# Register attention: the maxima are cut up straight behind the fourth one, and six kept products leave the similarity chain

## The chip, the cores and the metric

The kernel runs on one core of one Trainium2 chip. The metric is the device time of one execution in microseconds (us): the median of three executions of the kernel before was 1886.83 us (1886.52 to 1889.33). A core has five engines with an instruction queue each. TensorE (PE in the profile; PEld are its weight loads) multiplies matrices into PSUM banks. VectorE (DVE), ScalarE (ACT) and GpSimd (POOL) work on rows of 128 partitions. SyncE (SP) issues the large transfers. Each queue is worked off in the written order, and the queues meet only at semaphores.

## The reference, cut to what matters

The model is a four-layer decoder on 16 sequences of 128 tokens with 128 features and 16 heads of 8 features. The change lies in one of thirteen blocks, the "ffn" of layer 0, which is an attention with 5 register tokens (B is 16 and N is 128 here):

```python
qkv = (x @ W_qkv).reshape(Bx, Nx, 3, H, D)
q, k, v = (qkv[:, :, 0], qkv[:, :, 1], qkv[:, :, 2])
...
sim = (qg_n[None, None] * q_n).sum(-1).mean(-1)
sim = (sim - sim.min()) / (sim.max() - sim.min())
pos = sim > 0.9
logits = jnp.einsum('bqhd,bkhd->bhqk', q * scale, k)
...
reg_out = (x_pos[:, :REG] + x_neg[:, :REG]) * 0.5
tok_out = jnp.where(pos[:, :, None, None], x_pos[:, REG:], x_neg[:, REG:])
```

Each token is similar or not to one given query, after a minimum and a maximum over all tokens of all sequences. Each ordinary token attends to the registers and the tokens of its own side. The registers attend to both sides separately, and the two results are averaged. So no score of this block can be masked before the similarities of all 16 sequences are known.

## The kernel before, in words

All 16 sequences stay in SBUF. The blocks follow one another; each has one function per engine (`satt_pe`, `satt_act`, `satt_dve`, `satt_pool` for the five attention blocks, called with the block's name), and the order on every engine is written out by hand.

**The similarity chain** (`sim_pe`, `sim_act`, `sim_pool`, `sim_dve`) stands between the block before (cross-attention, S_X0) and the register attention (S_REG). The sequences form four groups of four. For each group TensorE turns x, multiplies it by the query weights, and ScalarE, GpSimd and VectorE make squares, products and sums of them. After the last group VectorE has the mean similarities; then a ping-pong of small operations between VectorE and TensorE follows. TensorE turns the columns (L1468), turns the extremes (L1471), spreads them to all partitions (L1474), and turns the masks (L1481). VectorE's step ahead of each adds one to `sim_mid`, TensorE's answer adds one to `sim_rows`. The masks end in `side_T` (L1623).

**Kept products.** q, k and v of all sequences are computed once by group: three products per group (`keep(g, m)`), each one PSUM bank of 128x512, which ScalarE copies to SBUF (L1503, semaphore `kept_sb`). L1451 is the form with one 512-column product (q and k, the weights standing still), L1454 the one with four 128-column products (v). Products 0 to 5 belong to groups 0 and 1 (sequences 0 to 7), 6 to 11 to groups 2 and 3. TensorE's queue mixes products 6 to 11 with the small operations of the chain, and ScalarE copies them in the same order. Two banks take turns, so product c waits for the copy of product c-2. GpSimd then spreads each group's queries of the registers into `reg_rows` (L1537).

**The attention loop** (`att_steps`, k from -2 to 17) works on several sequences at a time. In step k TensorE first multiplies the cut-up maxima of sequence k (`maxima_T`, L665, which waits for `m_cut`), computes the turned scores (L671, L675), turns the register row of k+1 (L748), subtracts the maxima (`fold_T`, L690, waits for ScalarE's copy `m_rows`, L811), computes the scores of k+1 (L644, L653), the values of k (L703), and so on down to the output projection of k-1 (L732, L358).

VectorE's step ends with the maxima of k+1 (four L873), and in this block alone with a register part: it waits for `reg_ps`, masks the register values (L912, L914), takes the register maximum (L920) and scales it (L922), for which ScalarE's exponential of the register rows (L847) waits. The next step begins with `cut_up(k)` (L879, L881): the four maxima are written as a bf16 number and its bf16 remainder, and `m_cut` is raised. ScalarE's step begins with the copy `m_rows` (L811); the register exponential stands last in its step, ahead of the next step's `m_rows` copy.

GpSimd makes the masked queries of sequence k+2 (`wides`, L537, after the values of k), a side mask (`side`, L548), and one exponent per sequence (L544).

Of the kernel before, what the change touches and what calls it, by code (L numbers as in the profile page):

```python
# [26 lines left out]
ALU = mybir.AluOpType  # L27
# [104 lines left out]
def decoder(nc, x_tok, x_T, ctx_tok, ctx_T, mask, mask_row, w_early, w_late, w_last, w_rest, bias, cols, rows,  # L132
            const, out, last=S_MOE):
    ctx = ExitStack()
    with ctx:
# [387 lines left out]
        def satt_pool(pool, sub, kind):  # L523
# [31 lines left out]
            for k in att_steps():  # L555
                if sub == S_MQA and has(k + 1):
                    wides(k + 1)
                if has(k - 2):
                    finish(k - 2)
                    if sub == S_X0 and k - 2 >= BATCH - 2:  # L560
                        sim_product(pool, k - BATCH)
                if sub != S_MQA and has(k + 2):
                    wides(k + 2)
                if sub == S_REG and has(k + 4):
                    side(k + 4)

        def satt_pe(pe, sub, kind, W, name, bias_name, mask_kind, out_w=384, out_name=None):
# [95 lines left out]
            def maxima_T(n):  # L663
                pe.wait_ge(m_cut, of_run(st, n))
                nc.tensor.matmul(ps[(n + 1) % 2][2][:, 0:128], m_cols[n % 2][:, :], ident_b[:, :], start=True,  # L665
                                 stop=True, skip_group_check=True).then_inc(mT_ps, 1)
# [70 lines left out]
            def reg_scores(n):  # L737
# [6 lines left out]
                                        skip_group_check=True)  # L744

            def reg_turn(n):
                pe.wait_ge(reg_e, n + 1)
                nc.tensor.transpose(ps[n % 2][1][:, 128:128 + REG_ROWS], reg_(n, "x")[0:REG_ROWS, :],  # L748
                                    ident[0:REG_ROWS, 0:REG_ROWS]).then_inc(reg_T, 1)
# [7 lines left out]
            for k in att_steps():  # L757
# [27 lines left out]
                if sub == S_REG and k + 1 < BATCH:  # L785
                    if has(k + 1):
                        mm = reg_values(k + 1)
                    if has(k + 2):
                        mm = reg_scores(k + 2)
                    mm.then_inc(reg_ps, 1)  # L790
                if sub == S_X0 and k == BATCH - 2:
                    sim_turn(pe, 0, ps[0][1])
# [11 lines left out]
        def satt_act(act, sub, kind):  # L804
            a, st = att_run[sub], st_run[sub]

            for k in att_steps():
# [24 lines left out]
                if has(n):  # L832
# [3 lines left out]
                    else:  # L836
# [6 lines left out]
                        v = v_part(sub, n)  # L843
                    nc.scalar.copy(own_heads(s)[:, :, 0:HD], v.rearrange("p (h d) -> p h d", h=HEADS)).then_inc(v_sb, 1)
                if sub == S_REG and has(n):
                    act.wait_ge(reg_m, n + 1)
                    nc.scalar.activation(reg_(n, "x")[0:REG_ROWS, :], ps[n % 2][1][0:REG_ROWS, 0:128], ACT.Exp,  # L847
                                         bias=reg_(n, "m2", 1)[0:REG_ROWS, :], scale=SCALE,
                                         accum_out=v_(s, ATT, "m2", 1, 1)[0:REG_ROWS, :]).then_inc(reg_e, 1)
                if sub == S_X0 and k == BATCH - 2:  # L850
                    sim_turned(act, 0, ps[0][1])
# [3 lines left out]
        def satt_dve(dve, sub, kind):  # L855
# [68 lines left out]
            for k in att_steps():  # L924
                if has(k):
                    cut_up(k)
                if sub == S_MQA and has(k + 1):
# [13 lines left out]
                if has(k + 1):  # L941
                    maxima(k + 1, 2, 4)
                if sub == S_REG and k + 1 < BATCH:
                    dve.wait_ge(reg_ps, k + 3)
# [480 lines left out]

        kept_bank = (ps[1][1], ps[1][2])
        sim_bank = ps[1][3]
# [7 lines left out]
        def sim_query(pe, g, bank):  # L1435
# [4 lines left out]
            mm.then_inc(sim_q, 1)  # L1440

        def sim_pe(pe):
            def keep(g, m):
                c = 3 * g + m
                if c == 0:
                    pe.wait_ge(oT_sb, of_run(att_run[S_X0], BATCH - 1))
                if c > 1:
                    pe.wait_ge(kept_sb, c - 1)
                bank = kept_bank[c % 2]
                if m < 2:  # L1450
                    mm = nc.tensor.matmul(bank[:, :], WA[:, W_EARLY("reg", 128 * m, 128)], sim_xT(g), start=True, stop=True)  # L1451
                else:
                    for q in range(4):
                        mm = nc.tensor.matmul(bank[:, 128 * q:128 * q + 128], sim_xT(g)[:, 128 * q:128 * q + 128],  # L1454
                                              WA[:, W_EARLY("reg", 256, 128)], start=True, stop=True, skip_group_check=True)
                mm.then_inc(kept_ps, 1)

            pe.wait_ge(sim_copy, 1)
            sim_query(pe, 2, ps[0][2])
            for m in range(3):  # L1460
                keep(0, m)
            sim_turn(pe, 3, ps[0][3])
            pe.wait_ge(sim_copy, 2)
            sim_query(pe, 3, ps[0][1])
            for m in range(3):
                keep(1, m)
            pe.wait_ge(sim_mid, 1)
            nc.tensor.transpose(sim_bank[0:16, 0:128], small[:, 48:64], ident).then_inc(sim_rows, 1)  # L1468
            keep(2, 0)
            pe.wait_ge(sim_mid, 2)  # L1470
            nc.tensor.transpose(sim_bank[0:2, 128:144], small[0:16, 64:66], ident[0:16, 0:16]).then_inc(sim_rows, 1)  # L1471
            keep(2, 1)
            pe.wait_ge(sim_mid, 3)
            nc.tensor.matmul(sim_bank[:, 144:146], ones_f[0:2, :], small[0:2, 68:70], start=True, stop=True,  # L1474
                             skip_group_check=True).then_inc(sim_rows, 1)
            keep(2, 2)
            keep(3, 0)
            keep(3, 1)
            pe.wait_ge(sim_mid, 4)
# [3 lines left out]
            mm.then_inc(sim_rows, 1)  # L1483
            keep(3, 2)

# [4 lines left out]
        def sim_squared(act, g, bank):  # L1490
# [5 lines left out]
            nc.scalar.copy(sim_(g, "q"), bank[:, :]).then_inc(sim_copy, 1)  # L1496

        def sim_act(act):
            def keep(g, m):
                c = 3 * g + m  # L1500
                act.wait_ge(kept_ps, c + 1)
                at = QKV_KEPT + 1536 * (g % 2) + 512 * m
                nc.scalar.copy(arena[g // 2][:, at:at + 512], kept_bank[c % 2][:, :]).then_inc(kept_sb, 1)  # L1503

            def root(h):
# [8 lines left out]
            for m in range(3):  # L1514
                keep(0, m)
            root(0)
            sim_turned(act, 3, ps[0][3])
            sim_squared(act, 3, ps[0][1])
            root(1)
            for c in range(3, 12):  # L1520
                keep(c // 3, c % 3)

        def sim_product(pool, g):
            pool.wait_ge(sim_copy, g + 1)
            if g > 1:
# [3 lines left out]
                                    ALU.mult).then_inc(sim_dot, 1)  # L1529

        def sim_pool(pool):
            sim_product(pool, 2)
            sim_product(pool, 3)
            for g in range(4):
                pool.wait_ge(kept_sb, 3 * g + 1)
                q = arena[g // 2][:, QKV_KEPT + 1536 * (g % 2):QKV_KEPT + 1536 * (g % 2) + 512]
                nc.gpsimd.tensor_tensor(  # L1537
                    reg_rows[:, 4 * REG_ROWS * g:4 * REG_ROWS * (g + 1)].rearrange("p (b h r) -> p b h r", b=4, h=HEADS),
                    heads(q)[:, :, 0:REG].unsqueeze(2).broadcast_to([128, 4, HEADS, REG]),
                    cst("headmask").unsqueeze(1).unsqueeze(3).broadcast_to([128, 4, HEADS, REG]),  # L1540
                    ALU.mult).then_inc(reg_q, 1)

# [1764 lines left out]
```

## Time and profile before

| what | value |
|---|---|
| median of 3 executions | 1886.83 us (1886.52 to 1889.33) |
| the profiled execution's own time | 1885.41 us |
| its span | 1883.6 us (1.8 us lie around it) |
| mean granted TensorE clock | 0.874 of full speed |
| TensorE busy | 1539.7 us (82%) |
| VectorE busy | 1108.1 us (59%) |
| ScalarE busy | 875.9 us (46%) |
| GpSimd busy | 610.5 us (32%) |
| similarity chain and hand-over | about 396 to 429 us from the start |
| register attention loop | about 429 to 558 us |

A row of the timeline gives start, duration, engine, line, operation, what it writes and reads, and how many were merged; in brackets stands how long the engine idled before it and who released it. A row of the waits gives the total wait, how many, and the longest. In a row of windows the busy time of an engine is followed by its number of instructions; the granted clock stands after the engines, 1.00 for 2.4 GHz and 0.50 for 1.2 GHz.

### The profile page before, as it was taken

How to read it: one execution, taken by the hardware profiler on the slowest of the kernel's cores; microseconds unless marked ns; L12 is line 12 of the kernel's file. 1: busy time of each engine (PE TensorE's matmuls, PEld its weight loads, DVE VectorE, ACT ScalarE, POOL GpSimd, SP SyncE). 2: the span in 40 equal slices, each digit the busy share in tenths (PEclk: the TensorE clock that was granted, in tenths of full speed). 3: DMA queues.
4: the chain of work that ended last, by engine and by line, in shares of the span. 5: the costliest groups of instructions: out<-in, count | busy, mean ns of one | idle time of the engine just before them, and what ended most of it. 6: DMA issues, size and time to landing. Idle time of an engine off the chain costs nothing.

```text
span 1883.6 us, 42915 instructions
## 1 busy us (share of the span) xinstructions
PE 1539.7 (82%) x15909; PEld 1010.8 (54%) x15916; DVE 1108.1 (59%) x3614; ACT 875.9 (46%) x2556; POOL 610.5 (32%) x849
## 2 busy tenths in 40 slices
PE   4556379978889777898889733699799999998998
PEld 3334246545656465455557412466477777776443
DVE  3434545555656657314767688566566666664776
ACT  2222334454546444344546544343366666666443
POOL 1422231132225533101222233212144444443666
PEclk6555579999999998999999855799899999999999
DMA  6000000000000000000020000000000000000000
GB/s 228 2 1 2 1 1 2 2 1 2 2 2 2 2 0 1 1 1 2 3 116 2 24 1 1 1 2 2 24 1 1 0 0 0 0 0 1 1 12 12
DMA packets 3605, 21.53 MB, mean 11 GB/s; under 512 B 1129, under 2 KB 1385, under 8 KB 2025
## 3 DMA queue, kind: packets, MB, share of 16 engines
q1 hardware_dynamic: 3434, 19.22, 2.7%
q8 instruction: 110, 1.80, 0.4%
q14 instruction: 61, 0.50, 0.1%
HBM read 18.15 MB, written 1.05 MB: 10 GB/s over the span
## 4 chain that ended last, share of the span: by engine, by line
PE 65%; DVE 12%; issue 7%; ACT 6%; POOL 4%; DVEq 3%; POOLq 1%; DMA 0%; ACTq 0%; another core or an unknown queue 0%; SPq 0%
PE ps L703 5%; PE ps L671 5%; PE ps L644 5%; PE ps L2459 4%; PE ps L2810 3%; PE ps L2469 3%; PE ps L2483 3%; PE ps L2438 3%; PE ps L2445 3%; PE ps L2282 2%; PE ps L1244 2%; PE ps L604 2%; PE ps L713 2%; PE ps L690 2%; PE ps L660 2%
## 5 line engine op out<-in xcount | busy, mean ns | idle before, releaser
L873 DVE TENSOR_REDUCE arena<-ps 128x4 f32<-128x512 f32 x320 | 204.3, 684 | 142.8 <-PE ps L660 73.6
L818 ACT ACTIVATE arena<-ps 128x512 f32<-128x512 f32 x320 | 171.7, 597 | 125.6 <-PE ps L690 123.4
L537 POOL TENSOR_TENSOR arena<-arena,C 128x512 f32<-128x512 f32 x80 | 83.1, 1040 | 428.3 <-ACT arena L839 137.4
L2375 POOL TENSOR_TENSOR arena<-arena 128x512 f32<-128x512 f32 x128 | 132.7, 1042 | 224.6 <-DVE arena L2684 224.1
L1244 PE MATMUL ps<-hid,WA 128*20 128x16 f32 x1024 | 57.1, 196 | 87.7 <-DVE hid L1295 87.7
L2602 ACT COPY arena<-ps 128x512 f32<-128x512 f32 x128 | 69.1, 588 | 123.2 <-PE ps L2469 123.2
L2593 ACT ACTIVATE arena<-ps,arena 128x256 f32<-128x256 f32 x256 | 119.9, 477 | 11.8 <-issue 8.1
L2810 PE MATMUL ps<-WA,maskadd 128*128 128x512 f32 x256 | 119.8, 598 | 1.8 <-DVE arena L2953 1.8
L703 PE MATMUL ps<-arena 128*32 128x128 f32 x2560 | 110.7, 282 | 3.2 <-ACT arena L818 3.0
L644 PE MATMUL ps<-arena 32*128 32x128 f32 x2560 | 104.7, 290 | 9.3 <-POOL arena L537 6.8
L2676 DVE TENSOR_REDUCE arena<-ps 128x2 f32<-128x512 f32 x128 | 82.5, 686 | 45.1 <-PE ps L2459 43.7
L1244 PEld LDWEIGHTS ps<-hid,WA 128*20 128x20 f32 x1024 | 43.5, 116 | 109.9 <-DVE hid L1295 109.4
L544 POOL TENSOR_TENSOR arena<-arena,C 128x1 f32<-128x1 f32 x80 | 43.7, 547 | 169.7 <-DVE arena L387 169.7
L3020 POOL TENSOR_TENSOR arena<-arena 128x256 f32<-128x256 f32 x112 | 82.2, 737 | 46.6 <-DVE arena L2953 36.9
L644 PEld LDWEIGHTS ps<-arena 32*128 32x128 f32 x2560 | 90.3, 195 | 12.8 <-POOL arena L537 8.0
L671 PE MATMUL ps<-arena 32*128 32x512 f32 x640 | 93.9, 657 | 0.0
L2876 ACT ACTIVATE arena<-ps 128x256 f32<-128x256 f32 x128 | 48.7, 383 | 72.8 <-PE ps L2810 49.8
L703 PEld LDWEIGHTS ps<-arena 128*32 128x32 f32 x2560 | 57.3, 109 | 39.0 <-issue 15.3
L1287 DVE SCALAR_TENSOR_TENSOR prod<-gates 20x32 f32<-20x32 f32 x128 | 23.0, 180 | 90.4 <-ACT gates L1270 90.4
L2469 PE MATMUL ps<-C,arena 128*128 128x128 f32 x512 | 70.7, 280 | 3.7 <-POOL arena L2375 3.7
L2459 PE MATMUL ps<-arena 64*128 64x256 f32 x512 | 72.6, 402 | 0.0
L2483 PE MATMUL ps<-arena 128*64 128x128 f32 x1024 | 70.3, 279 | 2.3 <-ACT arena L2602 2.3
(455 smaller groups left out, 3824.8 us busy)
## 6 DMA issues: line engine op xcount, KB each, us to landing
WA<-w_late SPq DMA_DIRECT2D x1, 4228.0 KB, 13.8
WA<-w_early SPq DMA_DIRECT2D x1, 1600.0 KB
R<-rows SPq DMA_DIRECT2D x1, 1282.0 KB, 7.2
WB<-w_rest SPq DMA_DIRECT2D x1, 1152.0 KB, 11.5
xT_all<-x_T SPq DMA_DIRECT2D x1, 1024.0 KB, 6.3
x_all<-x_tok SPq DMA_DIRECT2D x1, 1024.0 KB, 13.8
arena<-mask SPq DMA_DIRECT2D x1, 1024.0 KB
ctxT_all<-ctx_T SPq DMA_DIRECT2D x1, 1024.0 KB
```

The source lines that it names most:

```text
L644: mm = nc.tensor.matmul(ps[z][t][:, 128 * j:128 * j + 128], v_(z, ATT, "P", WIDE_Q + 128 * j, 128)[rows(t), :], keys_of(n)[rows(t), :], st ...
L671: nc.tensor.matmul(ps[s][t][:, :], keys_of(n)[rows(t), :], v_(s, ATT, "P", WIDE_Q, 512)[rows(t), :], start=True, stop=False, skip_group_ch ...
L703: mm = nc.tensor.matmul(ps[s][2][PAD * j:PAD * (j + 1), t * 128:(t + 1) * 128], va[:, 4 * t + j, :], v_(s, ATT, "PT", 128 * (4 * t + j), 128),
L818: nc.scalar.activation(v_(s, ATT, "PT", 512 * t, 512), ps[s][t][:, :], ACT.Exp, scale=SCALE).then_inc(pT_sb, 1)
L873: nc.vector.tensor_reduce(v_(z, ATT, "m", 4 * t, 4), heads(ps[z][t][:, :]), AXX, ALU.max)
L1244: mm = nc.tensor.matmul(bank(k // HALF, gt)[:, k % HALF, :], W_of(*weights("hh", gt)), h, start=False, stop=True, skip_group_check=True)
L2375: nc.gpsimd.tensor_tensor(p, p, v_(z, LAT, "rec", 4 * u + 2 * x, 2).unsqueeze(2).broadcast_to([128, 2, 256]), ALU.mult).then_inc(l_sub, 1)
L2459: mm = nc.tensor.matmul(score_bank(u, x)[:, 256 * j:256 * j + 256], v_(z, LAT, "qT", 128 * (2 * u + j), 128)[rows, :], kT[rows, 2 * u + j, :],
L2469: mm = nc.tensor.transpose(score_bank(u, x)[:, 128 * c:128 * c + 128], P_of(s, u, x)[:, 128 * c:128 * c + 128], ident)
L2483: mm = nc.tensor.matmul(half_bank(u)[XD * x:XD * x + XD, at:at + 128], V[:, k, 4 * u + 2 * j + x, 0:XD], PT_of(s, u, x)[:, 256 * j + 128 * ...
L2593: nc.scalar.activation(P_of(z, u, x)[:, 256 * j:256 * j + 256], score_bank(u, x)[:, 256 * j:256 * j + 256], ACT.Exp, scale=-1.0, bias=v_(z ...
L2810: nc.tensor.matmul(e_banks[m % E_BANKS][:, :], xT_of(n), WA[:, W_LATE("experts", FF * e, FF)], start=True, stop=True).then_inc(e_ps, 1)
```

## The change

Two things are changed, both in this block alone.

1. `cut_up` is called straight behind the maxima of the same sequence, at the end of VectorE's step, instead of at the beginning of the next. Only where something stood between the two does the order of instructions change; that is S_REG, where the wait for `reg_ps` and the register part stood there. In the four other attention blocks the same instructions follow one another as before.

2. Products 6 to 11 leave the similarity chain. TensorE computes 6 and 7 at the end of what it does in step -2 of the loop (behind the register scores of sequence 0), 8 to 11 in step -1 (behind the register scores of sequence 1). ScalarE copies 6 and 7 behind the register exponential of sequence 0, 8 to 11 ahead of that of sequence 1. From product 6 on `ps[1][3]` takes the place of `ps[1][1]`. TensorE waits for all twelve copies ahead of `maxima_T(0)`. GpSimd makes the register queries of groups 2 and 3 at the end of its steps 0 and 1. No transfer is added or moved.

```diff
@@ satt_pool
                 if sub == S_REG and has(k + 4):
                     side(k + 4)
+                if sub == S_REG and k in (0, 1):
+                    reg_queries(pool, k + 2)
@@ satt_pe
             def maxima_T(n):
                 pe.wait_ge(m_cut, of_run(st, n))
+                if sub == S_REG and n == 0:
+                    pe.wait_ge(kept_sb, kept_count(S_REG, BATCH - 1, 2))
...
+            def reg_keep(k):
+                if k == -2:
+                    for m in range(2):
+                        keep_pe(pe, 2, m)
+                elif k == -1:
+                    keep_pe(pe, 2, 2)
+                    for m in range(3):
+                        keep_pe(pe, 3, m)
...
                     mm.then_inc(reg_ps, 1)
+                    reg_keep(k)
@@ satt_act
+                if sub == S_REG and k == -1:
+                    keep_act(act, 2, 2)
+                    for m in range(3):
+                        keep_act(act, 3, m)
                 if sub == S_REG and has(n):
                     act.wait_ge(reg_m, n + 1)
...
+                if sub == S_REG and k == -2:
+                    for m in range(2):
+                        keep_act(act, 2, m)
@@ satt_dve
             for k in att_steps():
-                if has(k):
-                    cut_up(k)
...
                 if has(k + 1):
                     maxima(k + 1, 2, 4)
+                    cut_up(k + 1)
                 if sub == S_REG and k + 1 < BATCH:
                     dve.wait_ge(reg_ps, k + 3)
@@ sim_pe and its helpers
-        kept_bank = (ps[1][1], ps[1][2])
+        def kept_bank(c):
+            return (ps[1][1] if c < 6 else ps[1][3], ps[1][2])[c % 2]
...
-            keep(2, 0)
             pe.wait_ge(sim_mid, 2)
...
-            keep(2, 1)
             pe.wait_ge(sim_mid, 3)
...
-            keep(2, 2)
-            keep(3, 0)
-            keep(3, 1)
             pe.wait_ge(sim_mid, 4)
...
-            keep(3, 2)
@@ sim_act
-            for c in range(3, 12):
-                keep(c // 3, c % 3)
+            for m in range(3):
+                keep_act(act, 1, m)
@@ sim_pool
-            for g in range(4):
+            for g in range(2):
+                reg_queries(pool, g)
```

`keep_pe`, `keep_act` and `reg_queries` are the old bodies of `keep` and of GpSimd's loop, moved out unchanged but for the bank.

## Rows read from the trace of the kernel before

**Rows 1.** Windows of TensorE: a half-speed stretch; the steady loop (busy, count, clock).

```profile
412.80:415.90 3.10, 3.10 (x9) 0.50 0.00 0
438.40:543.00 104.60, 92.32 (x1482) 1.00 0.01 2
```

**Rows 2.** Waits of TensorE between 438.4 and 550.4 us.

```profile
PE ps L665 <- DVE m_cols L881: 11.4, 14, 1.1
```

**Rows 3.** Timeline, one steady step of the register loop.

```profile
470.44 0.23 PE L665 MATMUL ps<-ident_b,m_cols 128*128 128x128 bf16 x1 [0.75 <-DVE m_cols L881]
472.10 0.40 PE L690 MATMUL ps<-m_rows,pick_b 32*128 32x128 bf16 x8
...
475.48 1.28 DVE L873 TENSOR_REDUCE arena<-ps 128x4 f32<-128x512 f32 x2
...
476.22 1.04 POOL L537 TENSOR_TENSOR arena<-arena,C 128x512 f32<-128x512 f32 x1 [3.52 <-PE ps L703]
...
476.85 0.16 DVE L912 RECIPROCAL arena<-arena 80x1 f32<-80x1 f32 x1
...
477.24 0.61 POOL L548 TENSOR_SCALAR arena<-arena,C 128x128 bf16<-128x128 bf16 x1
...
477.46 0.22 PE L358 MATMUL ps<-bias,ones_b 128*128 128x128 bf16 x1
...
477.89 0.36 ACT L847 ACTIVATE arena<-ps,arena 80x128 f32<-80x128 f32 x1 [1.00 <-DVE arena L922]
477.94 0.17 DVE L879 CAST m_cols<-arena 128x16 bf16<-128x16 f32 x1
478.15 0.19 ACT L847 ACTIVATION_READ_ACCUMULATOR arena<-ps,arena 80x1 f32 x1
...
478.42 0.23 PE L665 MATMUL ps<-ident_b,m_cols 128*128 128x128 bf16 x1 [0.74 <-DVE m_cols L881]
```

**Rows 4.** Timeline of a later attention block (S_SELF2), where the cut follows the maxima.

```profile
914.58 1.04 POOL L537 TENSOR_TENSOR arena<-arena,C 128x512 f32<-128x512 f32 x1 [2.23 <-PE ps L703]
...
915.32 0.33 DVE L879 CAST m_cols<-arena 128x16 bf16<-128x16 f32 x1
...
915.82 0.25 DVE L888 RECIPROCAL arena<-ps 128x16 f32<-128x16 f32 x1
...
916.23 0.27 ACT L811 CAST m_rows<-ps 128x128 bf16<-128x128 f32 x1 [0.97 <-PE ps L665]
...
916.66 0.10 PEld L690 LDWEIGHTS ps<-m_rows,pick_b 32*128 32x128 bf16 x2 [0.23 <-ACT m_rows L811]
```

**Rows 5.** Timeline of the first stage: VectorE beside a TENSOR_SCALAR of GpSimd.

```profile
53.66 0.64 POOL L1109 TENSOR_SCALAR maskadd<-arena 128x128 bf16<-128x128 int32 x1 [1.39 <-DVE hid L1295]
53.76 0.34 DVE L1061 TENSOR_TENSOR arena<-R 128x128 f32<-128x128 f32 x1 [0.18 <-issue]
```

**Rows 6.** Timeline, the end of the similarity chain and the first two steps.

```profile
412.45 1.91 PE L1451 MATMUL ps<-xT_all,WA 128*128 128x512 f32 x2
...
412.80 0.22 DVE L1591 TENSOR_SCALAR small<-C,small 2x2 f32<-2x2 f32 x1
...
414.29 0.58 PE L1474 MATMUL ps<-small,arena 2*128 2x2 f32 x2
...
416.39 1.97 PE L1451 MATMUL ps<-xT_all,WA 128*128 128x512 f32 x4
...
420.30 1.28 ACT L847 ACT_TABLE_LOAD   x1
...
420.83 0.15 DVE L922 TENSOR_SCALAR arena<-arena 80x1 f32<-80x1 f32 x1
...
422.87 2.09 PE L644 MATMUL ps<-arena 32*128 32x128 f32 x32 [0.47 <-issue]
...
429.34 0.23 PE L665 MATMUL ps<-ident_b,m_cols 128*128 128x128 bf16 x1 [2.71 <-DVE m_cols L881]
...
438.43 0.23 PE L665 MATMUL ps<-ident_b,m_cols 128*128 128x128 bf16 x1 [1.03 <-DVE m_cols L881]
```

More of the change, by code:

```diff
@@ L1440, in sim_query, with keep_pe @@
             mm.then_inc(sim_q, 1)
-        def sim_pe(pe):
[L1443 to L1456, printed above, removed]
+        def keep_pe(pe, g, m):
+            c = 3 * g + m
+            if c == 0:
+                pe.wait_ge(oT_sb, of_run(att_run[S_X0], BATCH - 1))
+            if c > 1:
+                pe.wait_ge(kept_sb, c - 1)
+            bank = kept_bank(c)
+            if m < 2:
+                mm = nc.tensor.matmul(bank[:, :], WA[:, W_EARLY("reg", 128 * m, 128)], sim_xT(g), start=True, stop=True)
+            else:
+                for q in range(4):
+                    mm = nc.tensor.matmul(bank[:, 128 * q:128 * q + 128], sim_xT(g)[:, 128 * q:128 * q + 128],
+                                          WA[:, W_EARLY("reg", 256, 128)], start=True, stop=True, skip_group_check=True)
+            mm.then_inc(kept_ps, 1)
+        def sim_pe(pe):
             pe.wait_ge(sim_copy, 1)
@@ L1460, in sim_pe @@
             for m in range(3):
-                keep(0, m)
+                keep_pe(pe, 0, m)
             sim_turn(pe, 3, ps[0][3])
@@ L1465, in sim_pe @@
             for m in range(3):
-                keep(1, m)
+                keep_pe(pe, 1, m)
             pe.wait_ge(sim_mid, 1)
             nc.tensor.transpose(sim_bank[0:16, 0:128], small[:, 48:64], ident).then_inc(sim_rows, 1)
-            keep(2, 0)
             pe.wait_ge(sim_mid, 2)
             nc.tensor.transpose(sim_bank[0:2, 128:144], small[0:16, 64:66], ident[0:16, 0:16]).then_inc(sim_rows, 1)
-            keep(2, 1)
             pe.wait_ge(sim_mid, 3)
@@ L1496, in sim_squared, with keep_act @@
             nc.scalar.copy(sim_(g, "q"), bank[:, :]).then_inc(sim_copy, 1)
-        def sim_act(act):
[L1499 to L1503, printed above, removed]
+        def keep_act(act, g, m):
+            c = 3 * g + m
+            act.wait_ge(kept_ps, c + 1)
+            at = QKV_KEPT + 1536 * (g % 2) + 512 * m
+            nc.scalar.copy(arena[g // 2][:, at:at + 512], kept_bank(c)[:, :]).then_inc(kept_sb, 1)
+        def sim_act(act):
             def root(h):
@@ L1514, in sim_act @@
             for m in range(3):
-                keep(0, m)
+                keep_act(act, 0, m)
             root(0)
@@ L1529, in sim_product, with reg_queries @@
                                     ALU.mult).then_inc(sim_dot, 1)
+        def reg_queries(pool, g):
+            pool.wait_ge(kept_sb, 3 * g + 1)
+            q = arena[g // 2][:, QKV_KEPT + 1536 * (g % 2):QKV_KEPT + 1536 * (g % 2) + 512]
+            nc.gpsimd.tensor_tensor(
+                reg_rows[:, 4 * REG_ROWS * g:4 * REG_ROWS * (g + 1)].rearrange("p (b h r) -> p b h r", b=4, h=HEADS),
+                heads(q)[:, :, 0:REG].unsqueeze(2).broadcast_to([128, 4, HEADS, REG]),
+                cst("headmask").unsqueeze(1).unsqueeze(3).broadcast_to([128, 4, HEADS, REG]),
+                ALU.mult).then_inc(reg_q, 1)
         def sim_pool(pool):
@@ L1533, in sim_pool @@
             sim_product(pool, 3)
-            for g in range(4):
[L1535 to L1541, printed above, removed]
+            for g in range(2):
+                reg_queries(pool, g)
         def sim_norms(dve, g):
```

## The prediction

> **What bounds the kernel now.** I looked first for stretches in which TensorE, at 82% the busiest engine, isn't busy, then at its waits, then at one step in order of time. The steady part of the register loop is such a stretch: TensorE works 92.32 of 104.60 us at the full granted clock [rows 1]. Its waits name the cause: L665, the product of the cut-up maxima, waits 14 times for VectorE's L881, 11.4 us in all, at most 1.1 us [rows 2]. The step shows why. The maxima end at 476.76 (475.48 + 1.28); the register part runs from 476.85 on, and only at 477.94 does the cut begin. TensorE is through with the old step at 477.68 (477.46 + 0.22) and starts the next one at 478.42, after 0.74 us of idling [rows 3]. The step lasts 7.98 us (470.44 to 478.42), of which TensorE needs 7.24.
>
> The other place is the chain ahead of it. At 413.02 (412.80 + 0.22) VectorE has the number that L1474 needs, but a kept product that began at 412.45 holds TensorE for 1.91 us, so L1474 starts at 414.29 [rows 6].
>
> **Part 1, the cut ahead of the register part.** Nothing is added: two VectorE instructions change place with four. TensorE's limit falls to its own work, 7.24 us a step. What is late next? I follow one turn from fold to fold. The fold starts at 472.10, which I call F.
>
> - GpSimd's masked queries (L537) end at 477.26, F + 5.16 [rows 3].
> - The maxima end at F + 4.66, so the cast L879 now falls into that GpSimd operation. Where the cut already stands behind the maxima, the same cast, begun at 915.32, lasts 0.33 instead of 0.17 us and ends 0.03 us behind L537's end at 915.62; the next operation but one starts 0.17 us after it, at 915.82 [rows 4]. So here the cast ends at F + 5.19 and the register part starts at F + 5.36, where it would be F + 5.09 without the collision.
> - From the start of the register part (476.85) to that of the exponential (477.89) are 1.04 us, and to the end of its accumulator read another 0.45 (478.15 + 0.19 - 477.89) [rows 3]: F + 6.85.
> - ScalarE's queue is the new order's weak point. The `m_rows` copy, for which the fold waits, stands behind this exponential. Before, both became ready together; now the maxima's product is early and its copy waits for the register part. From the copy's start to the load of the fold's weights are 0.43 us (916.66 - 916.23) [rows 4]: F + 7.28.
>
> So the turn through VectorE and ScalarE takes 7.28 us and TensorE's own 7.24: the next limit is at the same place, and the step becomes 7.28. `m_cut` itself is ready in time: the cut's second half ends near 477.55, before TensorE is free at 477.68. The register turn (L748) needs the exponential some 0.2 us earlier than the fold does and also gets it. Behind the register part on VectorE now stands only what stood behind the cut before (the division), at the same hour; nobody waits for it within 1 us.
>
> From 438.43 to the product at 543.00 there are 13 steps in 104.57 us [rows 1, 6], 8.04 on average: the steps of 7.98 and two that are some 0.3 us longer by a delay on VectorE. That delay lies on the new turn, so I leave it in. 13 x 7.28 + 0.6 = 95.2; gain **9.4 us**. The last step has no register scores and no wait: 0.1 at most. Bounds: without the collision and the delays the steps are 7.24, 94.1, gain 10.5; if the second half of the cut is held too, see the second rival, gain 4.9.
>
> **Part 2, the six products.** Removed from the chain: L1474 starts at 413.08 instead of 414.29, 1.2 us; L1481 stands behind a product too, 0.3 us; ScalarE's 1.28 us table load, which today begins at 420.30 when the last copies are done, runs early, and the register exponential starts at the end of its maximum (420.98) rather than at 421.60: 0.6 us [rows 6]. Together **-2.1**.
>
> Added behind it: TensorE now has only the chain's four tiny jobs until the register scores of sequence 0, near 418.4. Today even with products in between the granted clock is at its lower level from 412.8 to 415.9, and with TensorE busy all through that stretch it is back at the full one for the products from 416.39 on [rows 1, 6]. I expect it low when products 6 and 7 come: 1.91 us each at that level, against 0.98 (1.97 for two) at the full one [rows 6]. With the copy of product 7 ahead of the register turn's copy on ScalarE, the scores of sequence 0 start near 424.1 rather than 422.87. By then, after 4 to 5 us of steady work, the clock should be up, and L644 takes some 1.2 instead of 2.09 us. Behind the register scores of sequence 1 come four products at about 1.0 us, to 430.4, and a copy of 0.6; so L665 of sequence 0 starts at 431.3 instead of 429.34, because it waits for all twelve copies. The first step ran at half speed for its first half (429.34 to 438.43, 9.09 us [rows 6]); now it takes 7.28 at the full clock and ends at 438.6. Net from 396 to the second L665: **+0.2 us**. So the chain's 2.1 us come back as work without cover. Ends: the clock never falls, -2.2; it stays low past both groups, +6.6, the four products at 1.9 to 2.0 us and the scores and first step as slow as today.
>
> GpSimd's two register queries (0.75 us each) move into steps 0 and 1 behind L548, ahead of a wait of some 3.5 us [rows 3]. ScalarE's six copies of 0.59 us are in the sum above. No DMA is issued, and no queue of SyncE is passed. The other four attention blocks keep their order.
>
> **Sum.** -9.4 - 0.1 + 0.2 = -9.3 us. The rows are of an execution of 1885.41 us, so 1876.1 for a like one; that execution is 1.4 us below the median shown, and the runs spread over 2.8 us, mainly by where the clock changes fall. On the median: **1877.5 us**.
>
> **Rivals.**
>
> *TensorE alone sets the step, and the clock holds.* For it: 7.24 and 7.28 are close, and the 0.43 us of the fold's start were measured where TensorE had other work in between. -10.5 - 0.1 - 2.2 = -12.8: 1874.0. Against: the cast's collision has a dozen like it in S_SELF2.
>
> *The cut's second half is held behind GpSimd's side mask.* L548 starts as L537 ends and lasts to 477.85, F + 5.75 [rows 3]; L881 falls into it. If held to its end, the register part starts near F + 5.70 and the turn is 5.70 + 1.04 + 0.45 + 0.43 = 7.62: 13 x 7.62 + 0.6 = 99.7, gain 4.9, in all -4.8: 1882.0. Against it: a two-input VectorE operation begun at 53.76 within a TENSOR_SCALAR of GpSimd (53.66 to 54.30) took 0.34 us, as long as such an operation takes alone [rows 5], and L548 is a TENSOR_SCALAR. The Trainium skill (SBUF — State Buffer, "Who interferes with whom") says that a VectorE instruction with two SBUF inputs contends with any GpSimd instruction that reads SBUF, and that the later one waits for the whole instruction. By that rule this rival is the forecast; the row of the first stage speaks the other way, that of the cast agrees.
>
> *Slower: the clock stays low.* Place: products 6 to 11, the scores of sequence 0 and the first step. Through the products alone it costs +6.6, so -9.5 + 6.6 = -2.9: 1883.9. It turns slower once the low level lasts into the full-length step behind: that one takes 14.5 instead of 7.3 us, and -2.9 + 6.1 (1.1 us of it are in the 6.6) makes +3.2 and, with the second step partly in it, about +4: 1891. For it: TensorE does next to nothing ahead of 418.4, where today six products lie. Against: the low stretch of today ended after 3 to 4 us of steady work [rows 1], and steady work begins at 418.5. The Trainium skill (TensorE: Matmul & The Clock Gate, "What's actually happening") says that the throttled clock is the default and activity releases it; it speaks against taking work out of the chain, and this rival is its price.
>
> *It doesn't do what it says:* `m_cut` early, but the register part on ScalarE keeps the fold where it was. The turn would have to take 0.7 us more than summed; then only the chain changes: -0.3 to +0.2, 1886.8.
>
> **Chances.** Forecast 0.70 (1875.5 to 1880.5 by itself); TensorE alone 0.12; second half held 0.08; clock low through the products 0.04, beyond 0.03; not what it says 0.03. The range goes from the first rival's time to just under that of the low clock: 1874.0 to 1883.5. A measurement of this kernel can tell about 0.2%, 3.8 us, from no change; below 1883.1 are the first three but for a part: 0.86 faster, 0.10 same, 0.04 slower.
>
> **What would show it.** Steps of 7.2 to 7.4 us between the L665; TensorE's wait for L881 gone and under 0.1 us of waiting for `m_rows` (L811) at L690; L879 at 0.4 us or more, ending with L537; L881 at 0.18 (if at 0.5, the second rival). L1474 at some 0.1 us behind L1591; a table load ahead of 412; products 6 and 7 near 1.9 us each and 8 to 11 near 1.0; the first L665 some 2 us later against L1591 than before, less 1.2. Wrong if the steps stay above 7.6 us, if L665 waits for copies beyond 3 us, or if the time leaves the range.

## The result

The changed kernel takes 1876.32 us (median of 6, 1873.68 to 1878.24) where the kernel before takes 1888.08 on the same chip (6 runs): ratio 0.9934 (0.9924 to 0.9945), 11.8 us less. A second series gave 0.9938 (0.9925 to 0.9952). The execution profiled after lasted 1875.85 us (span 1874.1, mean granted clock 0.872); the one of before 1885.41.

TensorE in the windows of [rows 1] (length, busy, granted clock), the 13 steps counted here from one cut-up product to the other:

```profile
412.80:415.90 3.10, 0.58 (x2) 0.50 0.00 0
438.18:532.63 94.45, 92.20 (x1482) 1.00 0.01 2
```

The same 13 steps took 104.57 us before, 94.45 now: -10.1. Of TensorE's waits between 438 and 539 us (total, times, longest) the one of [rows 2], now for L902, is left once as a wait of the product. The weight loads (PEld), which stand ahead of the products, show that a short wait for L902 is left in 12 steps:

```profile
PEld ps L761 <- ACT arena L865: 9.2, 14, 0.9
...
PEld ps L669 <- DVE m_cols L902: 3.1, 12, 0.5
...
PE ps L669 <- DVE m_cols L902: 0.3, 1, 0.3
```

The timeline of one steady step, to be laid beside [rows 3]:

```profile
480.27 1.04 POOL L537 TENSOR_TENSOR arena<-arena,C 128x512 f32<-128x512 f32 x1 [2.61 <-PE ps L707]
...
480.89 0.45 DVE L900 CAST m_cols<-arena 128x16 bf16<-128x16 f32 x1
...
481.29 0.61 POOL L548 TENSOR_SCALAR arena<-arena,C 128x128 bf16<-128x128 bf16 x1
481.42 0.27 DVE L902 TENSOR_TENSOR m_cols<-arena,m_cols 128x16 bf16<-128x16 f32 x1
481.52 0.22 PE L358 MATMUL ps<-bias,ones_b 128*128 128x128 bf16 x1
481.61 0.15 DVE L933 RECIPROCAL arena<-arena 80x1 f32<-80x1 f32 x1
481.74 0.23 PE L669 MATMUL ps<-ident_b,m_cols 128*128 128x128 bf16 x1
...
482.64 0.36 ACT L865 ACTIVATE arena<-ps,arena 80x128 f32<-80x128 f32 x1 [1.69 <-DVE arena L943]
...
482.90 0.19 ACT L865 ACTIVATION_READ_ACCUMULATOR arena<-ps,arena 80x1 f32 x1
483.00 0.25 ACT L825 CAST m_rows<-ps 128x128 bf16<-128x128 f32 x1
...
483.19 0.29 PE L761 MATMUL ps<-C,arena 80*128 80x80 f32 x1
483.41 0.40 PE L694 MATMUL ps<-m_rows,pick_b 32*128 32x128 bf16 x8
...
489.00 0.23 PE L669 MATMUL ps<-ident_b,m_cols 128*128 128x128 bf16 x1
```

The cut begins behind the maxima, its cast (L900) ends with GpSimd's L537, at 481.34 against 481.31, and the step is 7.26 us (489.00 - 481.74; 7.25 in most).

The timeline of the way into the loop, to be laid beside [rows 6]:

```profile
409.64 1.28 ACT L865 ACT_TABLE_LOAD   x1
...
413.02 0.22 DVE L1610 TENSOR_SCALAR small<-C,small 2x2 f32<-2x2 f32 x1
413.29 0.58 PE L1494 MATMUL ps<-small,arena 2*128 2x2 f32 x2 [0.55 <-DVE small L1610]
...
419.75 3.76 PE L1472 MATMUL ps<-xT_all,WA 128*128 128x512 f32 x4
...
424.48 1.17 PE L646 MATMUL ps<-arena 32*128 32x128 f32 x32 [0.89 <-ACT arena L1518]
...
427.56 1.97 PE L1472 MATMUL ps<-xT_all,WA 128*128 128x512 f32 x4
...
431.19 0.22 PE L669 MATMUL ps<-ident_b,m_cols 128*128 128x128 bf16 x1 [0.77 <-ACT arena L1518]
...
438.18 0.23 PE L669 MATMUL ps<-ident_b,m_cols 128*128 128x128 bf16 x1 [0.29 <-DVE m_cols L902]
```

Products 6 and 7 take 3.76 us at the lower level, products 9 and 10 1.97 at the full one. The granted clock is 0.50 in one piece from 409.8 to 423.3 us; before it was 0.50 in three shorter ones (412.8 to 416.0, 423.0 to 426.2, 429.8 to 433.0). The second cut-up product starts 0.25 us earlier than before. With the 13 steps (-10.1) and the last one (7.09 instead of 7.39) the stage is 10.7 us shorter. Behind it the same instructions of the two executions lie 12.8 us apart at 575 to 640 us of the execution before, 9.1 near 1314 and 9.7 at the end. The change touches none of these stages; in the first of them it is the granted clock that falls for longer before (559.4 to 569.7 us) than after (553.1 to 556.5). So a single execution tells no more than some 2 us, hence the medians.

### The profile page after: what moved, and what is told of

Read it like the earlier page. It is cut to its first block, busy times and chain, and to the rows that moved or that the text cites. A ratio compares the mean times of both kernels' runs of the same rounds, so it can differ in the third digit from the quotient of the medians.

```text
span 1874.1 us, 42923 instructions
## 1 busy us (share of the span) xinstructions
PE 1541.5 (82%) x15916; PEld 1011.6 (54%) x15916; DVE 1112.2 (59%) x3614; ACT 875.0 (47%) x2556; POOL 611.7 (33%) x849
## 4 chain that ended last, share of the span: by engine, by line
PE 67%; DVE 11%; issue 7%; ACT 6%; POOL 4%; DVEq 3%; POOLq 1%; DMA 0%; ACTq 0%; SPq 0%
PE ps L707 5%; PE ps L646 5%; PE ps L675 5%; PE ps L2829 4%; PE ps L2478 4%; PE ps L2488 3%; PE ps L2502 3%; PE ps L2457 3%; PE ps L2464 3%; PE ps L606 2%; PE ps L717 2%; PE ps L2301 2%; PE ps L1264 2%; PE ps L662 2%; PE ps L694 2%
## 5 line engine op out<-in xcount | busy, mean ns | idle before, releaser
L537 POOL TENSOR_TENSOR arena<-arena,C 128x512 f32<-128x512 f32 x80 | 83.2, 1041 | 420.2 <-ACT arena L853 138.6
L2612 ACT ACTIVATE arena<-ps,arena 128x256 f32<-128x256 f32 x256 | 120.1, 479 | 11.8 <-issue 8.1
L2972 DVE SCALAR_TENSOR_TENSOR arena<-ps,comb,arena 128x256 f32<-128x256 f32 x128 | 59.8, 480 | 20.7 <-ACT arena L2895 16.1
## 6 DMA issues: line engine op xcount, KB each, us to landing
WB<-w_rest SPq DMA_DIRECT2D x1, 1152.0 KB, 10.1
```

The source lines that it names most:

```text
L537: nc.gpsimd.tensor_tensor(heads(v_(n % 2, ATT, "P", WIDE_Q, 512)), src.unsqueeze(1).broadcast_to([128, 4, 128]), cst("tilemask").unsqueeze ...
L2612: nc.scalar.activation(P_of(z, u, x)[:, 256 * j:256 * j + 256], score_bank(u, x)[:, 256 * j:256 * j + 256], ACT.Exp, scale=-1.0, bias=v_(z ...
```

## The experiments

In three groups, each on one chip beside the kernel before. To compare kernels I give the ratio to before, with its 95% interval; 0.0010 is 1.9 us. "Ramp" is the time from the first of VectorE's two reciprocals of the similarity norms to the first cut-up product, in the profiled execution: 26.08 us before (403.26 to 429.34), 27.81 after (403.38 to 431.19). The low clock falls now ahead of the first cut-up product and now behind it, so a ramp is to be read together with the first step: 35.17 us before, 34.80 after.

**The two parts alone.** The first: `cut_up(k + 1)` moved as in the change, nothing else.

> The kernel before with the first part of the change alone: the cut of the fourth maxima stands behind the maxima, the twelve kept products stay in the similarity chain. My theory, from the two traces: nearly all of the gain is here. The steps of the register loop fall from 7.98 to 7.25 us, the wait of the cut-up maxima's product for VectorE is gone, and the stretch before the first step stays as it was before (TensorE's granted clock half in 412.8 to 415.9 and in parts of 422 to 433). Stage -10 us, -9.5 to -12 against the kernel before, 1876 to 1878.5 where before takes 1888. Rival, that the two parts need each other (kept products in the chain hold the first steps back so that the steps drift): -6 us or less, with steps above 7.5 us.

Measured: 0.9926 (0.9913 to 0.9940), 1875.24 us. Ramp 25.03, with the first step 33.39; in TensorE's timeline the steps are 7.25. The whole gain is here.

```profile
444.09 0.23 PE L665 MATMUL ps<-ident_b,m_cols 128*128 128x128 bf16 x1
451.34 0.23 PE L665 MATMUL ps<-ident_b,m_cols 128*128 128x128 bf16 x1
```

The second part alone, the products:

```diff
             for k in att_steps():
+                if has(k):
+                    cut_up(k)
...
                     maxima(k + 1, 2, 4)
-                    cut_up(k + 1)
```

> The changed kernel with the cut put back to the beginning of the step: the second part of the change alone. My theory: the steps stay at 7.98 to 8.04 us with a wait of about 0.7 us for VectorE in each, and what is ahead of them moves the second cut-up product by -0.3 to +0.3 us, so -2 to +2 us against the kernel before (clock placement in later stages included): same. Rival, that the products out of the chain carry a gain of their own which the changed kernel's ramp hides: -3 us or more.

Measured: 1.0016 (1.0007 to 1.0025), 1890.72 us: 3 us slower than before, where -2 to +2 was expected. The steady steps are 7.99 with 0.74 of waiting, as forecast; ramp and first step together are 35.47. In its profiled execution the clock stays low from 415 to 424, comes back, and falls once more in a full-length step, which takes 11.34 us (TensorE's timeline, 441.30 to 452.64):

```profile
441.30 0.23 PE L669 MATMUL ps<-ident_b,m_cols 128*128 128x128 bf16 x1 [1.50 <-DVE m_cols L902]
441.46 1.71 PE L675 MATMUL ps<-arena 32*128 32x512 f32 x8
...
444.44 2.09 PE L646 MATMUL ps<-arena 32*128 32x128 f32 x32
...
452.64 0.23 PE L669 MATMUL ps<-ident_b,m_cols 128*128 128x128 bf16 x1 [1.21 <-DVE m_cols L902]
```

So the second part brings nothing and may cost. Whether it costs anything beside the first part the runs don't settle: 0.9934 and 0.9938 against 0.9926 here, and 0.9921 against 0.9931 in the last group.

**How far the turn is from TensorE.** One extra VectorE reduction between cut and register part:

```diff
                     cut_up(k + 1)
+                if sub == S_REG and 0 <= k and k + 1 < BATCH:
+                    nc.vector.tensor_reduce(pad_out[:, :], R[:, ROWS("g_query")]...)
```

The reduction makes 128x16 of 128x128; its line is shortened here.

> The changed kernel with one extra VectorE reduction (128x128 to 128x16, about 0.3 us, as L382's kind of row gives) between the cut and the register part in 15 steps; nothing reads its result. It lengthens the turn through VectorE and ScalarE and leaves TensorE's work as it is. Theory of the prediction, corrected: TensorE's 7.25 us and the turn are within 0.1 to 0.2 us of each other, so of the 0.3 us some 0.1 to 0.2 us show in each step: steps 7.35 to 7.45, +1.5 to +3 us against the changed kernel, and TensorE's wait for the copy of the rows in ScalarE's queue appears. Rival, that TensorE's own work bounds the step and the turn has wide slack: steps stay at 7.25, 0 us.

Measured: 0.9952 (0.9937 to 0.9967); steps of 7.40 us. The expected place of the wait was wrong by one instruction: it is the register turn (L762 here) that comes late. VectorE's timeline in one step:

```profile
481.98 0.27 DVE L903 TENSOR_TENSOR m_cols<-arena,m_cols 128x16 bf16<-128x16 f32 x1
482.17 0.27 DVE L966 TENSOR_REDUCE pad_out<-R 128x16 f32<-128x128 f32 x1
482.37 0.14 DVE L934 RECIPROCAL arena<-arena 80x1 f32<-80x1 f32 x1
```

And TensorE's, where the register turn stands 1.59 us behind the cut-up product instead of 1.45:

```profile
482.31 0.23 PE L670 MATMUL ps<-ident_b,m_cols 128*128 128x128 bf16 x1
483.90 0.29 PE L762 MATMUL ps<-C,arena 80*128 80x80 f32 x1
489.71 0.23 PE L670 MATMUL ps<-ident_b,m_cols 128*128 128x128 bf16 x1
```

The reduction puts 0.39 us between the starts of L903 and L934 where there were 0.19: of 0.20 us, 0.15 show, so the branch through the register part had 0.05 us of slack. The timelines agree: the register turn starts 0.05 us behind the end of the accumulator read here (483.85), 0.10 behind it in the changed kernel (483.09).

Two of them:

> The changed kernel with two extra reductions instead of one between cut and register part. With one the steps are 7.40, so the turn is 0.15 us past TensorE's 7.25 and from there every bit of it shows: theory 7.40 + 0.28 = 7.68 us a step, +6 us against the changed kernel, and TensorE's product of fold weights waits for the copy of the rows. Rival, that the 0.15 us come from something else than the turn (the reduction disturbing TensorE's operands): 7.55 or less.

Measured: 7.59 us a step; 0.9948 (0.9930 to 0.9966, two runs, too few to part it from one reduction by time). The second adds 0.18 us of spacing (0.57 from L903 to L934) and 0.19 to the step: slope one. The expected 7.68 took the reduction's 0.28 us duration for what it adds to the queue. Of the wait for the copy of the rows that was expected there is none here either: the fold stands 0.22 us behind the register turn in every steady step, as in the changed kernel. TensorE's timeline now shows the wait for the exponential openly:

```profile
479.41 0.23 PE L670 MATMUL ps<-ident_b,m_cols 128*128 128x128 bf16 x1
481.20 0.29 PE L762 MATMUL ps<-C,arena 80*128 80x80 f32 x1 [0.27 <-ACT arena L866]
487.00 0.23 PE L670 MATMUL ps<-ident_b,m_cols 128*128 128x128 bf16 x1
```

**The cast's collision.** The stretched kernel with one reduction once more, GpSimd's masked queries held back:

```diff
                 if sub != S_MQA and has(k + 2):
+                    if sub == S_REG and has(k + 1):
+                        pool.wait_ge(m_cut, of_run(st, k + 1))
                     wides(k + 2)
```

> The one-reduction stretch of the turn again, with GpSimd's masked queries held until the cut of the same step is made, so that the cast no longer falls into that GpSimd operation. Theory: the cast is held by the GpSimd operation for some 0.28 us of its 0.45, and this is what brings the turn within 0.13 us of TensorE's 7.25 (with the stretch alone the steps were 7.40). Without the collision the turn has 0.4 us of slack, more than the reduction's 0.28: steps of 7.25 us again, cast 0.17 to 0.2 us. Rival, that the cast is long for another reason or that another VectorE operation runs into the later GpSimd operation instead: steps stay at 7.40 or more.

Measured: 0.9932 (0.9916 to 0.9947), the cast 0.17 us, and steps of 7.07, four of 7.15 to 7.28 among them. Both theories missed: the kernel with an added operation has shorter steps than the changed one. So 7.25 was never TensorE's own time. (L548 stands behind L537 in GpSimd's queue, so the wait moves it too, away from the second half of the cut.) The same wait alone, without the reduction:

> The changed kernel with GpSimd's masked queries held until the cut of the same step is made, nothing else. Theory A, from the stretched run (7.07 us a step although a reduction was added): the step of the changed kernel, 7.25 us, is set by the turn through VectorE, whose end is the cast held by the GpSimd operation, and TensorE alone would need 7.07 us; the 0.16 us wait hides in the modelled end of the bias product ahead of the cut-up product. So steps of 7.07 us, cast 0.17, the first cut-up product of a step 0.06 us behind the start of the bias product instead of 0.22; 14 x 0.18 = -2.5 us against the changed kernel. Theory B, the one on record for the stretch: TensorE's own work is 7.25 us, and this changes nothing (0 us; the 7.07 then came from the added reduction's shift of something).

Measured: 0.9921 (0.9908 to 0.9935), 1872.16 us; steps of 7.07, 13 of them in 92.12 us instead of 94.45, and a first step of 6.56 instead of 6.99. By time alone the intervals of the two kernels overlap; it is the steps that show the gain. Its timeline at the end of a step:

```profile
481.58 0.17 DVE L902 CAST m_cols<-arena 128x16 bf16<-128x16 f32 x1
481.83 0.18 DVE L904 TENSOR_TENSOR m_cols<-arena,m_cols 128x16 bf16<-128x16 f32 x1
...
482.08 1.04 POOL L537 TENSOR_TENSOR arena<-arena,C 128x512 f32<-128x512 f32 x1 [3.93 <-DVE m_cols L904]
...
482.20 0.22 PE L358 MATMUL ps<-bias,ones_b 128*128 128x128 bf16 x1
482.26 0.22 PE L671 MATMUL ps<-ident_b,m_cols 128*128 128x128 bf16 x1
```

Here the cut is made by 482.01, and the cut-up product starts 0.06 us behind the start of the bias product L358. In the changed kernel it starts 0.22 behind it (481.52, 481.74), 0.05 behind the end of the cut (481.42 + 0.27): there it waits 0.16 us for VectorE, and the bias product's modelled end covers that wait. The wait of the weight load for the cut, 3.1 us in 12 steps above, is gone. Theory A holds.

The wait on the kernel with the cut alone:

> The kernel before with the cut moved and the masked queries held until the cut is made; all twelve kept products still in the similarity chain. Theory A: steps 7.07 us here too, -2.5 us against the cut alone, 1872.5 to 1876 where before takes 1888; against the same edit on the changed kernel it shows once more what the moved products are worth: -1.5 to +0.5 us for leaving them in the chain.

Measured: 0.9931 (0.9918 to 0.9945), 1872.90 us; steps of 7.07, 13 of them in 92.15 us. Its ramp is 25.35, but the first step took 9.20 us, its first part at half clock (34.55 together, against 33.39 in the cut alone). The time is inside the expected range. The 2.5 us that were expected against the cut alone don't show in it: its ratio is the higher one, with intervals that overlap.

**The clock ahead of the loop.** Five products of 512 columns on TensorE without use, two ahead of the wait for `sim_mid` 1, three ahead of that for 4:

```diff
+        def idle_work(n):
+            for _ in range(n):
+                nc.tensor.matmul(ps[0][2][:, :], WA[:, W_EARLY("reg", 0, 128)], sim_xT(0), start=True, stop=True)
...
+            idle_work(2)
             pe.wait_ge(sim_mid, 1)
...
+            idle_work(3)
             pe.wait_ge(sim_mid, 4)
```

> The changed kernel with five idle 512-column float products added on TensorE in the similarity chain (two ahead of the chain's first small job, three ahead of its last pair; their results are not used). They do no useful work and can only cost, unless the clock matters. Theory: of what the changed kernel loses ahead of its first step, the larger part is the half clock of 410 to 423 us; with work in the chain the clock is full, products 6 and 7 take 0.94 to 1.0 us instead of 1.88 and the first cut-up product starts near 429 instead of 431.19: -2 us. Rival: the small jobs wait for the idle products (0.5 to 1 us) and the clock falls anyway, as in the kernel before: 0 to +2 us, the first cut-up product at 431 or later.

Measured: 0.9928 (0.9914 to 0.9941), 1873.89 us; the ramp is 26.25 us instead of 27.81: 1.6 us back for work that does nothing (by time alone the intervals of the two kernels overlap). Ramp and first step together are 33.24, against 34.80. L1481 here is the added work, L1472 products 6 and 7, which run at the full level, as TensorE's timeline shows:

```profile
413.44 4.46 PE L1481 MATMUL ps<-xT_all,WA 128*128 128x512 f32 x6
...
419.91 1.98 PE L1472 MATMUL ps<-xT_all,WA 128*128 128x512 f32 x4
...
422.85 1.17 PE L646 MATMUL ps<-arena 32*128 32x128 f32 x32 [0.89 <-ACT arena L1524]
```

The kept products can be that work. Products 6 and 7 ahead of the wait for `sim_mid` 1, 8 to 10 ahead of that for 4, 11 in step -1; ScalarE copies 3 to 10 in the chain; the two banks as before:

```diff
+            keep_pe(pe, 2, 0)
+            keep_pe(pe, 2, 1)
             pe.wait_ge(sim_mid, 1)
...
+            keep_pe(pe, 2, 2)
+            keep_pe(pe, 3, 0)
+            keep_pe(pe, 3, 1)
             pe.wait_ge(sim_mid, 4)
```

> The changed kernel with five of the six moved products put back into the chain, but each behind the small TensorE job that the chain waits for and only where VectorE's part of the chain gives TensorE a gap: products 6 and 7 ahead of its first wait for the chain's middle, 8, 9 and 10 ahead of its fourth, product 11 in the step before the loop. Theory: the granted clock falls because TensorE does next to nothing from 410 to 418 in the changed kernel; with work there the scores of sequence 0 start near 421 instead of 424.48 and the first cut-up product near 425.5 to 427 instead of 431.19: -3 to -5.5 us against the changed kernel, steps still 7.25. Rival, that the chain's own waits set this stretch and products in it delay it as before: 0, with the small jobs of the chain starting 1 us later than in the changed kernel.

Measured: 0.9910 (0.9896 to 0.9924), 1871.11 us; ramp 22.88 us, 4.9 less than in the changed kernel (with the first step 29.87, also 4.9 less), and the clock full but for some 3 us each about 407 and 424. The profiled execution, at 1867.88 us, was the fastest of its five; by the medians the kernel is 5.2 us below the changed one on the same chip. TensorE's timeline:

```profile
411.69 0.28 PE L1482 MATMUL ps<-C,small 128*16 128x128 f32 x1 [0.20 <-DVE small L1595]
...
413.46 0.38 PE L1486 MATMUL ps<-small,arena 2*128 2x2 f32 x2 [0.55 <-DVE small L1605]
413.77 1.16 PE L1465 MATMUL ps<-WA,xT_all 128*128 128x128 f32 x8
414.76 1.97 PE L1462 MATMUL ps<-xT_all,WA 128*128 128x512 f32 x4
416.90 0.44 PE L1493 MATMUL ps<-C,arena 128*128 128x128 f32 x2 [0.17 <-DVEq L1634]
...
421.05 1.17 PE L646 MATMUL ps<-arena 32*128 32x128 f32 x32 [0.47 <-issue]
```

In this execution the small jobs still wait for VectorE, not behind a product. With the later masked queries:

> The kernel with five products in the gaps of the chain (b1_gaps, 0.991 of before) and the masked queries held until the cut is made. Theory: the two edits touch different stretches, so their gains add: steps 7.07 us, -2.5 us against b1_gaps, 1868 to 1870 where before takes 1888. Rival: the later masked queries collide with something in VectorE's register part, or the clock falls elsewhere: no gain.

Measured: 0.9898 (0.9883 to 0.9914), 1868.54 us: the fastest kernel here, 19 us under before. Ramp 22.98, steps 7.07, 13 of them in 92.12 us: in the steps the gain adds. By the ratios the difference to the one without is 2.3 us, and the intervals overlap.

And product 11 one step earlier:

> The same with product 11 one step earlier, where TensorE sits idle 1.1 us behind the register scores of sequence 0; in b1_gaps it stood behind those of sequence 1, at half clock (2.08 us), and the first cut-up product waited 0.77 us for its copy. Theory: the first cut-up product starts 0.8 to 1.5 us earlier against the chain's start and waits for VectorE's cut instead, -1 us against b2_gaps_wides. Rival: the copy of product 11 holds the register turn's copy in ScalarE's queue, or the scores of sequence 0, by as much: 0.

Measured: 0.9908 (0.9893 to 0.9924), 1870.34 us: no gain. The product itself takes 1.16 us there, and the first cut-up product now waits for VectorE's cut, as expected. But in the profiled execution the granted clock is low from 413 to 420 and from 423 to 433; the scores of sequence 0 take 2.09 us, and the first step 8.19 (TensorE's timeline):

```profile
421.50 1.16 PE L1467 MATMUL ps<-WA,xT_all 128*128 128x128 f32 x8
...
423.62 2.09 PE L648 MATMUL ps<-arena 32*128 32x128 f32 x32 [0.67 <-ACT arena L1515]
```

The first of the two low stretches shows the limit of filling the gaps. Products 8 to 10 take 5.5 us in it (413.80 to 419.29) where b1_gaps had 2.9 (413.77 to 416.73), and the turn of the masks, the chain's last small job, starts right behind them at 419.08 instead of 416.90. In b2_gaps_wides too it stands behind them without a wait (418.65).

The changed kernel itself, for the comparisons:

> The changed kernel itself on the same chip as the others, for direct comparison: 0.993 of the kernel before; steps 7.25 us.

Measured: 0.9938 (0.9925 to 0.9952), 1876.31 us; ramp 27.82, steps 7.25, one of 7.40.

## Why the prediction held, point by point

1876.3 measured, 1877.5 forecast, within its own range. Shown by experiment: the cut alone brings the gain, and the new step is set by a turn through VectorE with the cast held by GpSimd. Not as forecast is the branch of the turn that ends last; that the sum came out so near in spite of it is luck.

- **A turn with the held cast sets the new step: right. Its branch: wrong.** The cast takes 0.45 instead of 0.17 and ends with L537. The forecast let the turn run through the register part, the exponential and the copy of the rows to the fold, 7.28. What ends last is the other branch, from the cut straight to the cut-up product, 7.25; the register part's branch would give 7.20 at the register turn (from the stretch). The fold waits for the copy in none of the runs: it stands 0.22 us behind the register turn, after (483.19, 483.41) as before (471.88, 472.10). The two branches share the turn up to the cast and end 0.05 us apart, which is why 7.28 was close.
- **The single distances.** With F = 476.16 (483.41 - 7.25) the cast ends at F + 5.18 (5.19 forecast), the register part starts at 5.45 (5.36), because the second half of the cut was stretched by 0.09, and the copy of the rows starts at 6.84 (6.85), before the accumulator read ends. That the fold then comes at 7.25 is no check of the sum, since F was set by it.
- **The price of the collisions.** Cast with L537 and second half with L548 cost 0.18 us a step together, shown by moving both GpSimd operations away (7.25 to 7.07). What each costs alone was not run.
- **"TensorE's own, 7.24": wrong, and by luck without effect on the sum.** The 0.74 us of idling in [rows 3] begins at the modelled end of the bias product. TensorE could have gone on 0.06 us after that product's start: 477.52, not 477.68. The idling was 0.90, TensorE's own step 7.08, and the runs without collision show 7.07. The Trainium skill (Perfetto Trace Analysis, "Identifying the Most-Contended Engine") says that the busy share of matmuls is not a good measure of how close TensorE is to its limit, because pipelined instructions look smaller in the trace. Here it was an idle time, read from a product's modelled end, that misled, by 0.16 us. The first rival's bound (7.24, 1874.0) fell with it: the kernel without the collision is at 1872.2.
- **"`m_cut` itself is ready in time": wrong.** It was measured against that same end. The cut ends at 481.69, and TensorE was free at 481.58, 0.06 us behind the start of L358; the product starts at 481.74, 0.05 behind the cut. This is the branch that sets the step.
- **The mis-sized term: the delays on VectorE.** 95.2 us forecast for the 13 steps, 94.45 measured. 13 x 0.03 is the turn; the other 0.4 are the 0.6 us for two late steps: the profile after shows a first one of 7.30 and one of 7.47 behind one of 7.16, 0.2 us over 13 of 7.25, and not 0.6. The last step gave 0.3 instead of 0.1.
- **The second half held to the end of L548: refuted, but it isn't free.** L902 lasts 0.27 instead of 0.18 and ends at 481.69, L548 at 481.90; so it is in all 12 steps in which the two meet. The rule that the prediction cites from the Trainium skill (SBUF — State Buffer, "Who interferes with whom") would hold L902 until 481.90; this row disagrees. The cast has a single input, so that rule doesn't speak of it, though it was held. And the prediction's reading of [rows 5] was off: two-input operations of that size with no GpSimd operation beside them take 0.29 us (L1561 at 404.64), so the one of 0.34 was stretched too. A later block of the kernel before shows more: there the same instruction, L881, falls into L537, a GpSimd operation with two tensors as inputs, and is held to its end, 0.88 us instead of 0.18. VectorE's instruction is the same in both rows; the GpSimd operation differs.

```profile
971.41 1.04 POOL L537 TENSOR_TENSOR arena<-arena,C 128x512 f32<-128x512 f32 x1 [3.87 <-ACT arena L839]
971.59 0.88 DVE L881 TENSOR_TENSOR m_cols<-arena,m_cols 128x16 bf16<-128x16 f32 x1
```

- **The ramp: right in its parts.** L1494 0.05 us behind the end of L1610 (0.1 forecast), table load at 409.6, products 6 and 7 at 1.88 each (1.91), scores of sequence 0 at 424.48 (424.1), first cut-up product at 431.19 (431.3), first step 6.99 us (7.28). Net -0.25 against +0.2. That the second part brings nothing is confirmed by the cut alone, which is as fast without it.
- **The clock rival: not seen here, real elsewhere.** It had a chance of 0.07. In both profiled executions of the changed kernel the clock is back ahead of the scores of sequence 0. Of the five other kernels with the same products moved and nothing laid into the chain, two show it: with products only it falls once more in a full-length step (11.34 us), and with two reductions it is low from 413 to 430 (first cut-up product at 434.43). One execution each is too few for a rate.
- **The sum and the median.** -9.3 forecast, -11.8 on the medians (by the interval of the ratio 10.4 to 14.3 us, so the forecast gain is a little small), -9.6 between the two profiled executions. The stage gave 10.7; what the rest is made of, beyond where the clock falls in other stages, wasn't followed.

## What to carry to other kernels

When a wait is removed, compute the turn of every engine that takes part, with what runs beside each operation in its new place; the next limit is often there and within a few per cent. Take an engine's own time from the start-to-start distances of instructions that don't wait, not from modelled ends: here 0.16 us of a wait stood hidden in the end of a product, and a change that seemed to be worth nothing took 2.3 us off 13 steps. Work taken out of a chain that other engines set gained nothing here, because it had to be done right behind it. Laid into the chain's gaps, never ahead of a small job, it cost nothing while the clock was full, and the ramp was 4.9 us shorter; at half clock it no longer fits the gap and holds the next small job.

## What the runs showed of the hardware

- A cast of 128x16 on VectorE that begins within GpSimd's L537, which reads two tensors in SBUF, ends with it: up to 0.45 us instead of 0.17. All 28 such casts of the changed kernel end 0.03 us behind L537. When GpSimd starts behind the cast, it takes 0.17.
- A VectorE operation with two inputs in SBUF, 0.18 us by itself, is held to the end of L537 in the same way (0.88 us at 971.59), but beside GpSimd's TENSOR_SCALAR L548 only stretched to 0.27. Why the two differ, no run here shows.
- Five products that nobody reads made the ramp 1.6 us shorter in the profiled execution (26.25 against 27.81): the granted clock was 1.00 instead of 0.50 for products 6 and 7.
- A reduction of 0.27 us adds 0.18 to 0.20 us to VectorE's queue: in the timeline successive operations overlap, and their durations don't sum.
